# Hybrid attention in a decoder kernel: the output product of a batch's second half cut in two halves of 8 heads, in steps 3 and 4 of the next batch, in PSUM bank 7

## Chip, cores and metric

The kernel runs on one core of a Trainium2 chip. The metric is the device time of one execution in microseconds, lowest is best; several runs of each kernel are timed and their median is taken.

## What is computed

A two-layer decoder on x of shape (8, 256, 256). Six blocks, each on a layer-normed x and added back to it: a linear mixer, cross attention, a gated feed-forward, causal self attention, hybrid attention, and a mixture of experts. The change touches the fifth alone:

```python
# 16 query heads of 128, 4 key/value heads; T = 64 context tokens, L = 256 tokens
q = rope(rms_norm((x @ wq).reshape(B, L, 16, 128), q_norm_w))
k = rope(rms_norm((x @ wk).reshape(B, L, 4, 128), k_norm_w))
k_full = concat([rms_norm(ctx @ wk_ctx, k_norm_w), k]); v_full = concat([ctx @ wv_ctx, x @ wv])
scores = einsum("blhd,bmhd->bhlm", q, repeat(k_full, 4)) / sqrt(128) + mask
out = einsum("bhlm,bmhd->blhd", softmax(scores), repeat(v_full, 4)).reshape(B, L, 2048)
x = x + out @ wo          # the product this change moves: 2048 -> 256
```

## The kernel before

Each engine has a program of its own, written out by hand in order, and the engines meet at counting semaphores; nothing is scheduled by a tool. The phases run one after the other. The hybrid phase goes over the 8 batches in pairs (`over_pairs`: batch 0, then a loop of three rounds of two batches, then batch 7). In the functions `hybrid(b, par, nxt)`, one for each engine, a batch has 8 steps: step i = 4j + g treats token half j (128 rows) and key/value head g with its 4 query heads, numbered u = 8b + i over all batches. The batches are software-pipelined: in step i PE (TensorE) works at once on the raw queries of unit u+3, the transposed queries of u+2, the scores of u+1, the transposed probabilities of u-1 and the outputs of u-2, and in between on the keys and values of this batch and the next.

PE's order in a step (`hybrid` in the tensor block, L1861 on):

1. scores of u+1, tiles 0 and 1 (banks 3 and 4; wait on `e_mx`, DVE's maxima of the unit before, and on `e_qc`, ACT's copy of the turned queries);
2. a piece for the batch's keys or values in bank 2 (transposes of keys, `turn_keys`, in steps 5 and 6; a projection in step 3);
3. `raw_query(u+3)` in bank 1 (waits on `e_qa`, DVE's `rotate_query`, which reads that bank);
4. `outputs(u-2)` in bank 0;
5. a further piece in bank 2: in step 4 `hybrid_out(b-1, 1)`, in step 7 `hybrid_out(b, 0)`, the product with `wo` of the former batch's second half and of this batch's first half;
6. scores of u+1, tiles 2 and 3;
7. `turn_query(u+2)` in bank 2;
8. `turn_probs(u-1)` in banks 5, 6 and, from step 5 to step 0 of the next batch (units of j = 1), bank 7.

`hybrid_out` (L1800) is a chain of 16 products, one for each head, into `PS[:, 2, 0:D]`, and increments `e_y` at its end. As all the data is float32, each `product` (L1496, the helper through which nearly all matmuls go) is two MATMULs of the profile. DVE's `hybrid_finish` (L739) waits for `e_y`, adds the 128 x 256 sum to x (L742) and increments `s_x` for j = 1. Only then may bank 2 be written again: PE waits for `s_x` in step 4 before `turn_query`.

DVE's order in a step (`hybrid` in the vector block, L745 on): `turned_probs(u-2)` (L735 to L737), `masked_max(u+1)` of tiles 0 and 1 (L716), `finish_query(u+2)` (L698, L702), `normalise(u)` (L725, L728), the keys' pieces (`square_key` L600 in steps 2 to 4; `turn_key` L611 to L625, two of three in step 4 and one in step 5, for the next batch), in step 4 `hybrid_finish(b-1, 1)`, then `masked_max(u+1)` of tiles 2 and 3 (L716, L721), then `rotate_query(u+3)` (L686, L692). In batch 7 there is no next batch, so no keys' pieces. Batch 0 has no former batch, so no `hybrid_out(b-1, 1)`. After batch 7 the last `hybrid_out(7, 1)` stands alone. ACT copies the turned queries (L1364) and probabilities (L1380), takes the exponentials (L1373) and the squares (L1357), and copies the outputs into `eOT` (L1387). POOL computes the norms' scales.

Of the kernel before, what the change touches and what calls it, by code (L numbers as in the profile page):

```python
# [5 lines left out]
B, S, D = 8, 256, 256  # L6
P = 128
# [7 lines left out]
XH, XG, XD = 16, 4, 128  # L15
# [18 lines left out]
MIX, CROSS, FFN, SELF, HYBRID, MOE = range(6)  # L34


def decoder_kernel(nc, I, out, rows, results):
    F32, BF, U8, U32 = mybir.dt.float32, mybir.dt.bfloat16, mybir.dt.uint8, mybir.dt.uint32
    ALU, ACT, AX = mybir.AluOpType, mybir.ActivationFunctionType, mybir.AxisListType
    ds = bass.ds  # L40

    with ExitStack() as ctx:
# [3 lines left out]
        def sem(name):  # L46
            return ctx.enter_context(nc.semaphore(name))
# [43 lines left out]
        wo = sb("wo", [P, XH, D])  # L91
# [44 lines left out]
        PS = ctx.enter_context(nc.psum_tensor("PS", [P, 8, 512], F32))  # L136
# [16 lines left out]
        s_x = sem("s_x")  # L153
# [137 lines left out]
        eOT = cut(0, (XH, S), F32, early)  # L291
# [26 lines left out]
        f_slot = small[:, 264:280]; f_slotu = small[:, 280:296].bitcast(U32)  # L318
        f_tiles = small[0:NE, 296:297]; f_incl = small[0:NE, 297:298]
        f_ex = small[0:1, 304:304 + TILES]; f_exu = small[0:1, 368:368 + TILES].bitcast(U32)  # L320

        mark = {}

# [2 lines left out]
        def _(dve):  # L326
# [27 lines left out]
            def tokens(b, j):  # L354
                return X[:, ds(b, 1), j, :].rearrange("p a d -> p (a d)")
# [383 lines left out]
            def hybrid_finish(b, j):  # L739

                dve.wait_ge(e_y, J * b + j + 1)
                dve.tensor_tensor(tokens(b, j), tokens(b, j), PS[:, 2, 0:D], ALU.add)\  # L742
                    .then_inc(s_x if j else e_yf, 1)

            def hybrid(b, par, nxt):  # L745
# [139 lines left out]
            for b in range(B):  # L885
                for j in range(J):
                    i = J * b + j
# [606 lines left out]
        def _(pe):  # L1494
            def product(dst, lhs, rhs, first=True, last=True):
                return pe.matmul(dst, lhs, rhs, start=first, stop=last)  # L1496
# [31 lines left out]
            for c in range(C):  # L1528
                last = product(PS[:, 3 + c, 0:D], b_fold[:, c * P:(c + 1) * P], c_fold[:, :])
# [149 lines left out]
            def keys(b, par, k, at=2):  # L1679

                if k:
                    pe.wait_ge(s_xt, HYBRID * B + b + 1)
                else:
                    pe.wait_ge(e_ct, b + 1)
                for c in range(C):
                    if k:
                        last = product(PS[:, at, :], eXT[:, par, c, T + (k - 1) * P:T + k * P], wk[:, c, :],
                                       c == 0, c == C - 1)
                    else:
                        product(PS[T:P, at, :], eCT[:, c, :], wvc[:, c, :], c == 0, c == C - 1)  # L1690
                        last = product(PS[0:T, at, :], eCT[:, c, :], wkc[:, c, :], c == 0, c == C - 1)
                last.then_inc(e_k, 1)
# [102 lines left out]
            pe.wait_ge(d_yb, B - 1)  # L1795
            project_out(B - 1)

            def hybrid_out(b, j):

                pe.wait_ge(e_oc, 8 * b + XG * (j + 1))  # L1800
                for h in range(XH):
                    last = product(PS[:, 2, 0:D], eOT[:, h, j * P:(j + 1) * P], wo[:, h, :], h == 0, h == XH - 1)
                last.then_inc(e_y, 1)

            def values(b, par, k):

# [12 lines left out]
            def turn_query(v, i):  # L1819
                pe.wait_ge(e_qf, v + 1)  # L1820
                for h in range(GH):
                    last = pe.transpose(PS[:, 2, h * P:(h + 1) * P], eQA[:, i % 2, h * XD:(h + 1) * XD], ident[:, :])  # L1822
                last.then_inc(e_qt, 1)
# [37 lines left out]
            def hybrid(b, par, nxt):  # L1861
                former = type(b) is not int or b > 0
                more = nxt[0] == HYBRID
                for i in range(8):
                    u = 8 * b + i
                    further = [i + k < 8 or more for k in range(4)]
                    pars = [par if i + k < 8 else 1 - par for k in range(4)]
                    if further[1]:
                        scores(u + 1, (i + 1) % 8, pars[1], (0, 1))
                    if i < 7:  # L1870
                        pe.wait_ge(e_qc, u + 2)
                    if i == 0:
                        values(b, par, 0)
                    if i == 2:
                        xt_turn(*nxt, 2)
                    if i == 3 and more:
                        keys(nxt[1], 1 - par, 2)
                    if i == 5 and more:
                        turn_keys(nxt[1], 0)
                    if i == 6 and more:  # L1880
                        turn_keys(nxt[1], 2)
                    if further[3]:
                        raw_query(u + 3, (i + 3) % 8, pars[3])
                    if i == 2:
                        pe.wait_ge(s_twice, 48 * b + 48)
                    if i >= 2:
                        outputs(u - 2, i - 2, par)
                    elif former:
                        outputs(u - 2, i + 6, 1 - par)
                    if i == 0:  # L1890
                        pe.wait_ge(e_vr, 2 * b + 1)
                        values(b, par, 1)
                    if i == 1 and more:
                        keys(nxt[1], 1 - par, 0)
                    if i == 2 and more:
                        keys(nxt[1], 1 - par, 1)
                    if i == 4 and former:
                        hybrid_out(b - 1, 1)
                    if i == 5 and more:
                        pe.wait_ge(e_kc, 3 * b + 4)  # L1900
                        turn_keys(nxt[1], 1)
                    if i == 7:
                        hybrid_out(b, 0)
                    if further[1]:
                        scores(u + 1, (i + 1) % 8, pars[1], (2, 3))
                    if further[2]:
                        if i == 0:
                            pe.wait_ge(e_vr, 2 * b + 2)
                        if i == 1 and more:
                            pe.wait_ge(e_kr, 3 * b + 4)  # L1910
                        if i == 2 and more:
                            pe.wait_ge(e_kr, 3 * b + 5)
                        if i == 2 and not more:
                            pe.wait_ge(s_xt, MOE * B + 1)
                        if i == 3 and more:
                            pe.wait_ge(e_kr, 3 * b + 6)
                        if i == 4 and former:
                            pe.wait_ge(s_x, HYBRID * B + b)
                        if i == 5 and more:
                            pe.wait_ge(e_kc, 3 * b + 5)  # L1920
                        if i == 6 and more:
                            pe.wait_ge(e_kc, 3 * b + 6)
                        if i == 7:
                            pe.wait_ge(e_yf, b + 1)
                        turn_query(u + 2, (i + 2) % 8)
                    if i >= 1 or former:
                        turn_probs(u - 1, (i - 1) % 8)

# [138 lines left out]
```

## Time and profile before

| | us |
|---|---|
| Median of 3 runs | 1327.38 (1327.04 to 1330.12) |
| Profiled execution, its own time | 1331.08 |
| Its span, first to last instruction | 1329.3 |
| PE busy | 1080.0 (81%) |
| DVE busy | 884.6 (67%) |
| ACT busy | 625.3 (47%) |
| POOL busy | 318.7 (24%) |
| Mean granted PE clock | 0.914 of full |

The difference of 1.8 us between the profiled execution's own time and its span lies before the first and after the last instruction. The hybrid phase is the stretch from about 494 to 1149 us of the span. It is highly regular: from batch 1 to batch 6 each takes 81.4 or 81.5 us in the timeline, with a granted clock of 1.00 throughout, and batch 7 ends at 1149. The parts of the page that average over the whole span say little of it, so the views used below are those of a stretch: the busy time by stretch, the waits, and the timeline of each engine, in which the same step of two batches can be laid side by side.

### The profile page before, as it was taken

Reading aid. Unit: us, or ns where it says so; the run is one execution under the profiler, and the core shown is the slowest. Engines: PE = TensorE matmul, PEld = TensorE weight load, DVE = VectorE, ACT = ScalarE, POOL = GpSimd, SP = SyncE. Lnnn points to the kernel's source line nnn. Section 1 sums busy time; section 2 is a strip of 40 time slices with the busy share of each in tenths; the row PEclk is TensorE's granted clock in tenths of the full one; section 3 lists DMA queues with packets and bytes.
Section 4 is the critical chain, followed back from the end, with each engine's and each line's share of the span. In section 5 each row is a group of like instructions: output and inputs, shape, how many; then the busy total and the mean of one; then the engine's idle time right before and its main releaser. Section 6 shows DMA issues by size and latency. Waiting matters only on the chain.

```text
span 1329.3 us, 22376 instructions
## 1 busy us (share of the span) xinstructions
PE 1080.0 (81%) x6416; PEld 743.4 (56%) x6417; DVE 884.6 (67%) x2462; ACT 625.3 (47%) x1971; POOL 318.7 (24%) x467
## 2 busy tenths in 40 slices
PE   3677777788999958899999999999999999543790
PEld 2453444566666635566656666566665667332680
DVE  4576657588778756968778687886868776152352
ACT  1435676455555615555565455655546464031230
POOL 1113222113111322313132131321413210014334
PEclk9955899999999978899999999999999999855795
DMA  9400000112211000000000000000000000431455
GB/s 320 157 0 33 0 1 0 49 50 61 83 47 47 18 1 13 1 13 1 1 13 1 13 0 4 9 0 13 0 7 6 0 13 1 131 122 48 134 120 142
DMA packets 44549, 55.58 MB, mean 42 GB/s; under 512 B 4657, under 2 KB 35249, under 8 KB 44209
## 3 DMA queue, kind: packets, MB, share of 16 engines
q1 hardware_dynamic: 38576, 46.28, 11.4%
q10 hardware_dynamic: 4352, 4.20, 1.6%
q0 software_dynamic: 1536, 4.20, 1.0%
q8 instruction: 28, 0.46, 0.1%
q14 instruction: 57, 0.46, 0.1%
HBM read 34.73 MB, written 16.78 MB: 39 GB/s over the span
## 4 chain that ended last, share of the span: by engine, by line
PE 42%; DVE 7%; issue 4%; ACT 4%; DMA 2%; POOL 2%; ACTq 1%; SPq 0%; DVEq 0%; POOLq 0%
PE PS L1496 38%; PE PS L1822 2%; DMA rows_dram<-cosT 1%; ACT arena L1364 1%; PE PS L1845 1%; POOL rows_dram L1134 1%; ACT arena L1373 1%; DVE arena L692 1%; POOL arena L1149 1%; DVE early L869 1%; DVE arena L716 1%; DVE arena L728 1%; PE PS L1506 1%; SPq L958 0%; ACT arena L1480 0%
## 5 line engine op out<-in xcount | busy, mean ns | idle before, releaser
L1496 PE MATMUL PS<-EW,arena 128*64 (+5 forms) x1024 | 181.3, 319 | 25.0 <-DVE small L716 11.9
L1496 PEld LDWEIGHTS PS<-EW,arena 128*128 128x128 f32 (+1 forms) x1024 | 141.6, 163 | 63.0 <-issue 33.4
L1496 PE MATMUL PS<-early,arena 128*32 128x128 f32 (+6 forms) x864 | 107.9, 362 | 33.3 <-DVE early L579 23.7
L1496 PE MATMUL PS<-wq,EW 128*128 128x512 f32 x256 | 127.4, 621 | 7.7 <-DVE arena L692 7.1
L1098 POOL TENSOR_SCALAR small<-small 128x4 f32<-128x4 f32 x64 | 25.3, 396 | 424.2 <-ACT mask L1357 352.3
L716 DVE CUSTOM_DVE_ANT_0 arena<-PS,kmask 128x128 f32<-128x128 f32 (+3 forms) x256 | 93.8, 389 | 42.4 <-PE PS L1496 32.4
L1373 ACT ACTIVATE arena<-arena,small 128x128 f32<-128x128 f32 (+3 forms) x256 | 119.4, 471 | 0.3
L1496 PE MATMUL PS<-wo,early 128*128 128x256 f32 x512 | 113.2, 380 | 0.8 <-ACT early L1387 0.8
L1364 ACT ACTIVATE arena<-PS 128x512 f32<-128x512 f32 x64 | 38.2, 597 | 157.2 <-PE PS L1822 157.2
L1496 PEld LDWEIGHTS PS<-wo,early 128*128 128x128 f32 x512 | 97.4, 190 | 14.1 <-issue 1.2
L1000 POOL TENSOR_SCALAR ve<-mv 128x2 f32<-128x2 f32 x48 | 10.6, 221 | 369.3 <-DVE mv L351 369.2
L1496 PEld LDWEIGHTS PS<-early,arena 128*32 128x32 f32 (+3 forms) x864 | 51.0, 116 | 85.2 <-issue 46.1
L647 DVE TENSOR_REDUCE small<-PS 128x4 f32<-128x512 f32 x64 | 58.2, 951 | 42.0 <-PE PS L1496 42.0
L1357 ACT ACTIVATE mask<-PS 128x128 f32<-128x128 f32 x256 | 66.5, 273 | 40.0 <-PE PS L1496 39.6
L1496 PEld LDWEIGHTS PS<-wq,EW 128*128 128x128 f32 x256 | 45.8, 194 | 55.4 <-issue 41.2
L1100 POOL TENSOR_TENSOR small<-small,halves 128x4 f32<-128x4 f32 x64 | 72.8, 1138 | 5.3
L728 DVE TENSOR_SCALAR arena<-arena,small 128x128 f32<-128x128 f32 (+3 forms) x256 | 68.8, 333 | 2.3
L1496 PE MATMUL PS<-arena,EW 128*128 128x512 f32 (+1 forms) x160 | 63.2, 509 | 2.1 <-ACT arena L1380 2.1
L1338 ACT ACTIVATE arena<-PS,small 128x256 f32<-128x256 f32 x128 | 63.0, 492 | 0.0
L1506 PE MATMUL PS<-ident,XN 128*128 128x128 f32 x160 | 32.5, 339 | 37.2 <-DVE XN L365 37.2
L1299 ACT ACTIVATE early<-PS 128x384 f32<-128x384 f32 x64 | 28.5, 488 | 71.4 <-PE PS L1726 71.4
L742 DVE TENSOR_TENSOR X<-X,PS 128x256 f32 (+1 forms) x16 | 6.7, 421 | 81.1 <-PE PS L1496 81.1
(251 smaller groups left out, 2401.8 us busy)
## 6 DMA issues: line engine op xcount, KB each, us to landing
EW<-in_masksT_dram SPq DMA_DIRECT2D x32, 256.0 KB, 3.4
results_dram<-EW SPq DMA_DIRECT2D x32, 128.0 KB, 3.2
EW<-results_dram SPq DMA_DIRECT2D x4, 1024.0 KB, 9.5
rows_dram<-cosT SPq DMA_DIRECT2D x1, 4096.0 KB, 19.3
arena<-rows_dram SPq DMA_DIRECT2D x16, 256.0 KB, 3.1
results_dram<-early ACTq DMA_DIRECT2D x16, 256.0 KB, 3.2
X<-in_x_dram SPq DMA_DIRECT2D x1, 2048.0 KB, 8.9
wq<-in_wq_dram SPq DMA_DIRECT2D x1, 2048.0 KB, 10.9
```

What stands on the lines that cost most here:

```text
L647: last = dve.tensor_reduce(d_neg[:, i % 2, j, :], PS[:, 0:4, at:at + n], AX.X, ALU.max, negate=True)
L716: dve.tensor_tensor_reduce(probs(i, t), PS[:, 3 + t % 2, 0:n], kmask[:, at:at + n], 1.0, LOWEST, ALU.add, ALU.max, e_max[:, t:t + 1]).then ...
L728: last = dve.tensor_scalar(probs(i, t), probs(i, t), e_inv[:, t:t + 1], None, ALU.mult)
L1100: pool.tensor_tensor(e_rqs[:, i % 2, :], e_q3[:, i % 2, :], halves[:, 0:GH], ALU.pow).then_inc(e_rq, 1)
L1299: act.activation(dPT[:, i % 2, r, :], PS[:, 4 + r, 0:3 * P], ACT.Copy).then_inc(d_pt, 1)
L1338: act.activation(dP[:, i % 2, r, P:3 * P], PS[:, r, P:3 * P], ACT.Exp, bias=d_neg[:, i % 2, 1, r:r + 1]).then_inc(d_e, 1)
L1357: last = act.activation(eSQ[:, h * XD:(h + 1) * XD], PS[:, 1, h * XD:(h + 1) * XD], ACT.Square, accum_out=e_q2[:, i % 2, h:h + 1])
L1364: act.activation(eQT.rearrange("p (t h q) -> p h t q", t=4, h=GH), PS[:, 2, :].rearrange("p (h t q) -> p h t q", t=4, h=GH), ACT.Copy).the ...
L1373: last = act.activation(tile, tile, ACT.Exp, bias=e_neg[:, i % 2, t:t + 1], accum_out=e_sum[:, i % 2, t:t + 1])
L1496: return pe.matmul(dst, lhs, rhs, start=first, stop=last)
L1506: last = pe.transpose(PS[:, to, at:at + P], XN[:, j, c * P:(c + 1) * P], ident[:, :])
L1822: last = pe.transpose(PS[:, 2, h * P:(h + 1) * P], eQA[:, i % 2, h * XD:(h + 1) * XD], ident[:, :])
```

## The change

The product of a batch's second half, `hybrid_out(b-1, 1)`, no longer stands as one chain of 16 heads in step 4. Heads 0 to 7 are done in step 3 and heads 8 to 15 in step 4, at the same place in the step (after `outputs`, before the scores of tiles 2 and 3), and they accumulate in bank 7. DVE's `hybrid_finish` reads bank 7. PE's wait for `s_x` moves from step 4, before `turn_query`, to step 5, before `turn_probs`, the next to write bank 7. The first half's product (step 7) and the very last one (after batch 7) stay whole and in bank 2. DVE's, ACT's and POOL's orders are unchanged.

```diff
+        def out_bank(b, j):
+            return 7 if j and (type(b) is not int or b < B - 1) else 2
...
                 dve.wait_ge(e_y, J * b + j + 1)
-                dve.tensor_tensor(tokens(b, j), tokens(b, j), PS[:, 2, 0:D], ALU.add)\
+                dve.tensor_tensor(tokens(b, j), tokens(b, j), PS[:, out_bank(b, j), 0:D], ALU.add)\
...
-            def hybrid_out(b, j):
+            def hybrid_out(b, j, heads=range(XH)):
...
-                for h in range(XH):
-                    last = product(PS[:, 2, 0:D], eOT[:, h, j * P:(j + 1) * P], wo[:, h, :], h == 0, h == XH - 1)
-                last.then_inc(e_y, 1)
+                for h in heads:
+                    last = product(PS[:, out_bank(b, j), 0:D], eOT[:, h, j * P:(j + 1) * P], wo[:, h, :],
+                                   h == 0, h == XH - 1)
+                if heads[-1] == XH - 1:
+                    last.then_inc(e_y, 1)
...
+                    if i == 3 and former:
+                        hybrid_out(b - 1, 1, range(XH // 2))
                     if i == 4 and former:
-                        hybrid_out(b - 1, 1)
+                        hybrid_out(b - 1, 1, range(XH // 2, XH))
...
-                        if i == 4 and former:
-                            pe.wait_ge(s_x, HYBRID * B + b)
...
+                    if i == 5 and former:
+                        pe.wait_ge(s_x, HYBRID * B + b)
                     if i >= 1 or former:
                         turn_probs(u - 1, (i - 1) % 8)
```

The instructions on PE, first in step 3 of a loop batch, from `outputs` to the scores of tiles 2 and 3 (`wo` and `early` are the operands of the output product, `EW` and `arena` of the scores and outputs; L1499 of the changed kernel is L1496 of the one before). Before:

```order
L1496 MATMUL PS<-arena,EW 128x512 [waits e_oc,e_pta]
L1496 MATMUL PS<-arena,EW 128x256 [waits e_ptd]
L244 REGISTER_ALU [waits e_qc]
L1496 MATMUL PS<-EW,arena 128x320 [waits e_mx]
L244 REGISTER_ALU
L1496 MATMUL PS<-EW,arena 128x64 [waits e_mx]
L1496 MATMUL PS<-EW,arena 128x256
```

and now:

```order
L1499 MATMUL PS<-arena,EW 128x512 [waits e_oc,e_pta]
L1499 MATMUL PS<-arena,EW 128x256 [waits e_ptd]
L1803 ISA
L1499 MATMUL PS<-wo,early 128x256 [waits e_oc]
L1499 MATMUL PS<-wo,early 128x256 x7
L244 REGISTER_ALU [waits e_qc]
L1499 MATMUL PS<-EW,arena 128x320 [waits e_mx]
L244 REGISTER_ALU
L1499 MATMUL PS<-EW,arena 128x64 [waits e_mx]
L1499 MATMUL PS<-EW,arena 128x256
```

Eight products of `wo` (one with its wait, and 7) now stand between the outputs and the scores of tiles 2 and 3 of step 3. In step 4, from `outputs` to the first row of `turn_query` (L1822, now L1827), before:

```order
L1496 MATMUL PS<-arena,EW 128x512 [waits e_oc,e_pta]
L1496 MATMUL PS<-arena,EW 128x256 [waits e_ptd]
L1800 ISA
L1496 MATMUL PS<-wo,early 128x256 [waits e_oc]
L1496 MATMUL PS<-wo,early 128x256 x15
L244 REGISTER_ALU [waits e_qc]
L1496 MATMUL PS<-EW,arena 128x320 [waits e_mx]
L244 REGISTER_ALU
L1496 MATMUL PS<-EW,arena 128x64 [waits e_mx]
L1496 MATMUL PS<-EW,arena 128x256
L1918 REGISTER_ALU
L1822 MATMUL PS<-ident,arena 128x128 [waits e_qf,s_x]
```

and now:

```order
L1499 MATMUL PS<-arena,EW 128x512 [waits e_oc,e_pta]
L1499 MATMUL PS<-arena,EW 128x256 [waits e_ptd]
L1499 MATMUL PS<-wo,early 128x256 [waits e_oc]
L1499 MATMUL PS<-wo,early 128x256 x7
L244 REGISTER_ALU [waits e_qc]
L1499 MATMUL PS<-EW,arena 128x320 [waits e_mx]
L244 REGISTER_ALU
L1499 MATMUL PS<-EW,arena 128x64 [waits e_mx]
L1499 MATMUL PS<-EW,arena 128x256
L1827 MATMUL PS<-ident,arena 128x128 [waits e_qf]
```

Of the 16 products 8 are left, and `turn_query` no longer waits for `s_x`. In step 5, `turn_query` and `turn_probs` (L1845 and L1847, now L1850 and L1852), before:

```order
L1822 MATMUL PS<-ident,arena 128x128 [waits e_qf,e_kc]
L1822 MATMUL PS<-ident,arena 128x128 x3
L1845 MATMUL PS<-ident,arena 128x128 [waits e_p]
L1845 MATMUL PS<-ident,arena 128x128 x7
L1847 MATMUL PS<-ident,arena 128x128
```

and now:

```order
L1827 MATMUL PS<-ident,arena 128x128 [waits e_qf,e_kc]
L1827 MATMUL PS<-ident,arena 128x128 x3
L1932 REGISTER_ALU
L1850 MATMUL PS<-ident,arena 128x128 [waits e_p,s_x]
L1850 MATMUL PS<-ident,arena 128x128 x7
L1852 MATMUL PS<-ident,arena 128x128
```

The wait for `s_x` now stands at `turn_probs`.

## Rows read from the trace of the kernel before

**Rows 1.** Busy time by stretch: batch 4 of the hybrid phase, and batch 7.

```profile
core 0: us, PE busy (x) PEld busy (x) DVE busy (x) ACT busy (x) POOL busy (x), PEclk, DMA share, GB/s
...
822.90:904.40 81.50, 78.27 (x348) 52.53 (x347) 62.63 (x196) 43.60 (x165) 21.18 (x27) 1.00 0.02 5
...
1067.30:1149.00 81.70, 77.75 (x356) 55.43 (x353) 48.68 (x172) 39.11 (x136) 7.47 (x12) 1.00 0.02 6
```

**Rows 2.** Waits of PE in the hybrid phase: us in total, times, longest.

```profile
PE PS L1496 <- DVE small L716: 5.4, 7, 0.9
```

**Rows 3.** Timeline, PE, steps 3 to 6 of one steady batch.

```profile
start us, us, engine line op out<-in xcount [idle before <-releaser]
857.62 1.36 PE L1496 MATMUL PS<-EW,arena 128*128 128x320 f32 x6
...
864.40 7.07 PE L1496 MATMUL PS<-wo,early 128*128 128x256 f32 x32
871.30 1.36 PE L1496 MATMUL PS<-EW,arena 128*128 128x320 f32 x6
872.50 0.60 PE L1822 MATMUL PS<-ident,arena 128*128 128x128 f32 x4
...
873.94 1.12 PE L1496 MATMUL PS<-EW,arena 128*128 128x256 f32 x4 [0.30 <-ACT arena L1364]
...
875.38 1.98 PE L1496 MATMUL PS<-wq,EW 128*128 128x512 f32 x4
...
882.59 1.13 PE L1496 MATMUL PS<-EW,arena 128*128 128x256 f32 x4 [0.87 <-DVE small L716]
...
884.56 1.99 PE L1496 MATMUL PS<-wq,EW 128*128 128x512 f32 x4 [0.41 <-DVE arena L692]
```

**Rows 4.** Timeline, DVE, the same steps.

```profile
859.88 0.69 DVE L686 TENSOR_TENSOR arena<-PS,cosq 128x512 f32<-128x512 f32 x1
...
869.14 0.69 DVE L625 TENSOR_TENSOR early<-early,small 128x512 f32<-128x512 f32 x1
871.62 0.42 DVE L742 TENSOR_TENSOR X<-X,PS 128x256 f32 x1 [1.79 <-PE PS L1496]
...
874.83 0.27 DVE L736 COPY arena<-PS 64x128 f32<-64x128 f32 x1
...
876.86 0.69 DVE L702 TENSOR_TENSOR arena<-arena,small 128x512 f32<-128x512 f32 x1
877.97 0.18 DVE L725 RECIPROCAL small<-small 128x4 f32<-128x4 f32 x1 [0.43 <-ACT arena L1373]
...
882.04 0.48 DVE L716 CUSTOM_DVE_ANT_0 arena<-PS,kmask 128x320 f32<-128x320 f32 x1
...
884.42 0.68 DVE L735 COPY arena<-PS 128x512 f32<-128x512 f32 x1
```

**Rows 5.** Timeline, PE then DVE, step 6: DVE's paces behind PE.

```profile
888.53 1.36 PE L1496 MATMUL PS<-EW,arena 128*128 128x320 f32 x6
...
887.04 0.69 DVE L702 TENSOR_TENSOR arena<-arena,small 128x512 f32<-128x512 f32 x1
887.65 0.17 DVE L725 RECIPROCAL small<-small 128x4 f32<-128x4 f32 x1
...
890.79 0.69 DVE L686 TENSOR_TENSOR arena<-PS,cosq 128x512 f32<-128x512 f32 x1
```

**Rows 6.** Timeline, ACT, step 5: end of the exponentials.

```profile
877.75 0.19 ACT L1373 ACTIVATION_READ_ACCUMULATOR arena<-arena,small 128x1 f32 x1
```

**Rows 7.** Timeline, PE, batch 0, where no output product covers step 4.

```profile
546.99 2.02 PE L1496 MATMUL PS<-EW,arena 128*128 128x256 f32 x4 [3.59 <-DVE small L716]
```

**Rows 8.** Busy time by stretch, columns as in Rows 1, around that wait.

```profile
543.50:547.00 3.50, 0.01 (x1) 0.04 (x1) 3.43 (x9) 0.53 (x1) 2.93 (x3) 1.00 0.00 0
547.00:550.00 3.00, 3.00 (x9) 2.06 (x10) 2.92 (x13) 0.34 (x2) 0.00 (x0) 0.50 0.00 0
```

**Rows 9.** Timeline, DVE, step 4 of batch 7.

```profile
1109.18 0.42 DVE L742 TENSOR_TENSOR X<-X,PS 128x256 f32<-128x256 f32 x1 [6.37 <-PE PS L1496]
```

## Prediction

> **What bounds the kernel now.** I read the busy time by stretch first. In a steady batch of the hybrid phase PE is busy 78.27 us of 81.50 at a granted clock of 1.00, DVE 62.63 [rows 1]. PE sets the end, and only its 3.2 us of idle time a batch could be won; any new wait of PE is paid in full. Next the waits: PE waited 5.4 us in total, 7 times, for L716, DVE's masked maxima [rows 2]. Laid beside the timelines, that is 0.87 us once in each of six batches, at the start of step 6 [rows 3], and a smaller one in batch 7. Last the timelines of steps 3 to 6. In step 4 PE's output product runs from 864.40 to 871.30 [rows 3], 32 MATMULs in 6.90 us, so 0.216 us each. Beside it DVE works off its longest step: it ends with the keys' L625 at 869.14, and then idles 1.79 us for the end of the product, until L742 at 871.62 [rows 4]. So here PE covers DVE with 1.79 us to spare. From L742 on DVE is the late one: PE waits for it at 882.59 (0.87 us) and 884.56 (0.41 us) [rows 3].
>
> **PE's work.** The change removes no product and adds none: 16 MATMULs, 3.45 us, go from step 4 to step 3, and the product's end stays where it was, at 871.30, if PE meets no new wait. Splitting the chain costs no visible time: neighbouring groups start at the same pace within and across pieces [rows 3]. The changed kernel has six more rows on PE in all; at 0 us, since PE's registers and waits are worked off beside the matmuls, as in the unbroken run from 864.40 to 872.50 [rows 3].
>
> **The wait for `s_x`.** What the move could win is a wait of PE before `turn_query` in step 4. L742 ends at 871.62 + 0.42 = 872.04 [rows 4], while PE is at its scores until `turn_query` at 872.50, which shows no idle time before it [rows 3]. The wait was met 0.46 us early: the gain is 0. In its new place, before `turn_probs` of step 5, it stands behind the raw query, which comes 2.4 us or more after L742 by the times below. The Trainium skill (Perfetto Trace Analysis, Optimizing Tensor Performance, Matmuls) says that independent matmul groups should rotate through banks so that reading one out overlaps the next group. By that rule the move to bank 7 would help; the row shows no wait for it to remove, so the sum holds nothing for it.
>
> **DVE's start into step 4.** This is where the change costs. DVE's `masked_max` of tiles 2 and 3 in step 3 waits for PE's scores, and these now stand behind the first half: they start at 857.62 + 3.45 = 861.07 instead of 857.62 [rows 3]. Where DVE waited for these scores, its `rotate_query` (L686) began 890.79 - 888.53 = 2.26 us after they did [rows 5]. So it begins at 863.33, against 859.88 before [rows 4]: 3.45 us later, the full half. It idles that long in step 3, to no use. From there to L625 DVE ran without a wait before, and everything PE feeds it with in step 4 is 3.45 later too; so L625 starts at 872.59 instead of 869.14 [rows 4]. The next instruction can start 0.61 us after a 512-wide one (887.04 to 887.65 [rows 5]): L742 at 873.20, not 871.62. The product has been complete since 871.3. DVE is **1.58 us later** than before, since the half that left step 4 took its cover along and gave it to a step in which DVE had nothing to do.
>
> **From there to PE.** Before, L742 to L736 took 874.83 - 871.62 = 3.21 us with two short waits for the scores in it [rows 4]. Those waits vanish. L742 takes 0.34 us (0.42 less the 0.08 by which the next instruction overlaps its end, as with L702, 0.69 long and 0.61 to the next [rows 5]), and L716 to the end of `rotate_query` takes 884.42 - 882.04 = 2.38 us when nothing waits [rows 4]. L736 is at 873.20 + 2.72 = 875.92: 1.09 us late. Two things follow.
>
> PE in step 5. The scores of tile 0 need the maxima of tile 2. PE started 882.59 - 882.04 = 0.55 us after that L716 began [rows 3, 4]; now 873.54 + 0.55 = 874.09 against 873.94, 0.15 us late. The next `raw_query` needs `rotate_query`: in step 6 it came 884.56 - 884.42 = 0.14 us after DVE's next instruction [rows 3, 4]; now 876.06 against 875.38, 0.68 us late.
>
> DVE in step 5. L702 is at 876.86 + 1.09 = 877.95, and L725 could follow at 878.56. It began at 877.97 before, waiting for ACT's exponentials, which ended at 877.94 [rows 4, 6]. These are fed by PE and come at most 0.15 us later, so they no longer hold DVE: of the 1.09 us, **0.59** are left. Then DVE runs without a wait to L716 at 882.04 [rows 4], which is what PE waits for at 882.59. So PE starts step 6 **0.59 us later** than before, and as both are late by the same from there on, and no wait of PE in the rest of the batch is for something that was early, nothing wins it back.
>
> **How often, and the sum.** Batches 1 to 6 have both a former batch and the next batch's keys: 6 x 0.59 = 3.5 us. Batch 0 has no former batch and is untouched. In batch 7 DVE has no keys' work and idles 6.37 us before L742 [rows 9]; losing 3.45 us of it costs 0. The profiled execution's 1331.08 us (span 1329.3) would become 1334.6; it lies 3.7 us over the median, and the same 3.5 us on the median of 1327.38 give **1330.9 us**.
>
> **Check and bounds.** Batch 0 is the same step 4 without any cover: there PE waited 3.59 us for L716 at 546.99 [rows 7]. Half the cover, 3.45 us, brings that to 0.14, and the L742 that batch 0 lacks adds 0.34: a wait of 0.48 us at the start of step 5. My reckoning above has the 0.30 that is there now plus 0.15. The two agree to 0.03. The unknown is how much of the 1.09 is absorbed. Low end: 0.4 a batch, if PE's paces to DVE are 0.2 shorter than taken, 6 x 0.4 = 2.4. High end: 0.83, if the register work before L742, hidden in my sum, shows and ACT takes the 0.15 as well, 5.0. So 1329.8 to 1332.4 for this case. About 0.3%, 4.0 us, is what a measurement of this kernel can tell from no change, so the case lies on both sides of that line.
>
> **Rivals.**
> - *Nothing moves* (0 us, 1327.4). For: 1.79 us of idle time stood before L742, and some slack may exist which the profile doesn't show, or DVE may begin its step 4 earlier than in lockstep. Against: DVE's row of instructions is in order behind the scores of step 3.
> - *Faster.* If the shorter stretches let DVE finish the sum earlier relative to PE, the waits of 0.87 and 0.41 us in step 6 would go: 6 x 1.28 = 7.7 us, 1319.7. It would need the product to be complete before DVE is free, and DVE free before 871.62. The first comes true, the second can't, unless DVE's keys' work runs in the time won in step 3, and it stands behind the scores there.
> - *Nothing absorbed.* If ACT is later too (it copies the keys that PE turns in step 5), DVE's 1.09 or even 1.58 us come through: 6.5 to 9.5 us, 1333.9 to 1336.9. Against: ACT's input is only 0.15 us late.
> - *The clock falls.* After the wait of 3.59 us in batch 0, PE idle in 543.5 to 547, the granted clock was 0.50 (1.2 GHz) in 547 to 550 [rows 8]. If step 5's new waits did the same in each batch, with some 3 us at half speed, 1.5 us a batch would be added: 3.5 + 9 = 12.5, 1339.9. It decides from the point at which the waits of steps 5 and 6 pull the clock below 1.00. Against: the waits of 0.87 and 0.41 us, 2 us apart, left it at 1.00 [rows 1, 3], and the new ones, 0.45 and 0.53 us, are smaller. The Trainium skill (Perfetto Trace Analysis, Matmul Optimizations) says that the engine scales its power with utilization, so matmuls should run back to back in batches; it speaks against cutting one in two. The rows keep 2.4 GHz through gaps of that size, so I give it little.
>
> **How the numbers follow.** The forecast has 0.62, of which 0.25 lie over the 4.0 us line and 0.37 under it. Nothing moves 0.14, faster 0.09, nothing absorbed 0.09, the clock 0.06. So faster 0.09; same 0.37 + 0.14 = 0.51; slower 0.25 + 0.09 + 0.06 = 0.40. The range leaves out the faster case, the clock and the upper part of the unabsorbed one: 1327.0 to 1334.0, with the unchanged time just inside.
>
> **What would show it.** In a batch like the one above: DVE idle some 3 us before L716 in step 3; no idle time before L742 in step 4; PE idle about 0.45 us at the start of step 5 and about 0.5 us before the raw query after it, where there was none; no wait of DVE for the exponentials in step 5; a batch of 82.1 us instead of 81.5; a clock of 1.00. The reasoning is wrong if DVE still idles before L742, if the period of a batch doesn't grow, or if batch 7 changes by more than 0.3 us.

## The result, and the profile after

| | before | after |
|---|---|---|
| Median | 1328.81 us (13 runs) | 1332.76 us (13 runs) |
| Lowest and highest | 1326.73, 1332.12 | 1329.01, 1335.66 |
| Profiled execution's span | 1329.3 | 1328.6 |
| From the first to the last L742 (now L745) | 570.94 us | 574.36 us |

The ratio is 1.0027, with a 95% interval of 1.0015 to 1.0040: slower by 2.0 to 5.3 us. The spans of the two profiled executions say nothing of it: the one of the changed kernel reached the hybrid phase 3.9 us sooner (its first L745 is at 573.8, the first L742 at 577.65), and nothing that the change touches comes before that point. Within the hybrid phase the comparison is sharp, since the batches repeat to 0.1 us. Taken from one sum of a first half to the next (L742, L745), each of the six batches 1 to 6 took 81.42 us on average before and 81.99 now, 0.57 more, and batch 7 took 66.34 both times.

The busy time by stretch after, batch 4 and batch 7 (columns as in [rows 1]: PE, PEld, DVE, ACT and POOL busy, PEclk):

```profile
821.00:903.00 82.00, 78.26 (x347) 52.32 (x345) 62.41 (x195) 43.82 (x165) 19.50 (x27) 1.00 0.02 5
...
1066.90:1149.00 82.10, 78.09 (x356) 55.58 (x354) 49.08 (x173) 39.11 (x136) 7.48 (x12) 1.00 0.03 6
```

PE is as busy in batch 4 as in [rows 1], in a stretch of 82.00 us instead of 81.50, at a granted clock of 1.00. The timeline of PE after, the same batch as in [rows 3]; its step 3 begins at 849.81 where that of before begins at 851.93, so 2.12 us are to be added for a comparison:

```profile
855.49 3.62 PE L1499 MATMUL PS<-wo,early 128*128 128x256 f32 x16
858.95 1.36 PE L1499 MATMUL PS<-EW,arena 128*128 128x320 f32 x6
...
865.73 3.62 PE L1499 MATMUL PS<-wo,early 128*128 128x256 f32 x16
869.18 1.36 PE L1499 MATMUL PS<-EW,arena 128*128 128x320 f32 x6
870.37 0.60 PE L1827 MATMUL PS<-ident,arena 128*128 128x128 f32 x4
...
871.96 1.13 PE L1499 MATMUL PS<-EW,arena 128*128 128x256 f32 x4 [0.44 <-DVE small L719]
...
873.93 1.98 PE L1499 MATMUL PS<-wq,EW 128*128 128x512 f32 x4 [0.45 <-DVE arena L695]
...
881.03 1.13 PE L1499 MATMUL PS<-EW,arena 128*128 128x256 f32 x4 [0.78 <-DVE small L719]
...
883.01 1.98 PE L1499 MATMUL PS<-wq,EW 128*128 128x512 f32 x4 [0.41 <-DVE arena L695]
```

And DVE's, as in [rows 4]:

```profile
859.85 0.49 DVE L719 CUSTOM_DVE_ANT_0 arena<-PS,kmask 128x320 f32<-128x320 f32 x1 [3.14 <-PE PS L1499]
...
861.21 0.69 DVE L689 TENSOR_TENSOR arena<-PS,cosq 128x512 f32<-128x512 f32 x1
...
870.47 0.69 DVE L628 TENSOR_TENSOR early<-early,small 128x512 f32<-128x512 f32 x1
871.08 0.41 DVE L745 TENSOR_TENSOR X<-X,PS 128x256 f32 x1
...
873.79 0.27 DVE L739 COPY arena<-PS 64x128 f32<-64x128 f32 x1
...
876.43 0.17 DVE L728 RECIPROCAL small<-small 128x4 f32<-128x4 f32 x1
...
880.49 0.48 DVE L719 CUSTOM_DVE_ANT_0 arena<-PS,kmask 128x320 f32<-128x320 f32 x1
```

The product now stands in two chains of 16 MATMULs, at 855.49 and 865.73. DVE waits 3.14 us for the scores of step 3 (L719 at 859.85), and up to the sum no more: `hybrid_finish` (L745) at 871.08 follows L628 with no idle time, where L742 waited 1.79 us in [rows 4]. PE waits 0.44 us for DVE at the start of step 5 (871.96) and 0.45 us before the raw query (873.93), where it had 0.30 and nothing; step 6 begins at 881.03, at 883.15 on the clock of before, 0.56 us late.

### The profile page after: what moved, and what is told of

Its sections match the earlier page's. It is cut to its first block, busy times and chain, and to the rows that moved or that the text cites. A ratio compares the mean times of both kernels' runs of the same rounds, so it can differ in the third digit from the quotient of the medians.

```text
span 1328.6 us, 22367 instructions
## 1 busy us (share of the span) xinstructions
PE 1075.8 (81%) x6407; PEld 741.0 (56%) x6417; DVE 883.4 (66%) x2462; ACT 626.7 (47%) x1971; POOL 308.9 (23%) x467
## 3 DMA queue, kind: packets, MB, share of 16 engines
q1 hardware_dynamic: 38576, 46.28, 11.4%
## 4 chain that ended last, share of the span: by engine, by line
PE 36%; DVE 10%; issue 10%; ACT 3%; POOL 1%; SPq 1%; DMA 1%; ACTq 0%; DVEq 0%; POOLq 0%
PE PS L1499 33%; DVE arena L719 1%; PE PS L1827 1%; DVE arena L695 1%; DVE arena L731 1%; PE PS L1850 1%; POOL arena L1152 1%; ACT arena L1367 1%; DVE early L872 1%; DVE arena L705 1%; DVE early L625 1%; DVE early L620 1%; DVE arena L701 1%; DVE early L616 1%; SPq L961 0%
## 5 line engine op out<-in xcount | busy, mean ns | idle before, releaser
L1499 PE MATMUL PS<-EW,arena 128*64 (+5 forms) x1024 | 181.1, 319 | 25.6 <-DVE small L719 14.0
L1499 PEld LDWEIGHTS PS<-EW,arena 128*128 128x128 f32 (+1 forms) x1024 | 141.0, 163 | 64.0 <-issue 33.6
L719 DVE CUSTOM_DVE_ANT_0 arena<-PS,kmask 128x128 f32<-128x128 f32 (+3 forms) x256 | 93.6, 389 | 63.6 <-PE PS L1499 54.6
L1499 PE MATMUL PS<-wq,EW 128*128 128x512 f32 x256 | 127.3, 620 | 10.4 <-DVE arena L695 9.8
L1499 PE MATMUL PS<-early,arena 128*32 128x256 f32 (+6 forms) x856 | 104.1, 358 | 34.1 <-DVE early L582 23.7
L1101 POOL TENSOR_SCALAR small<-small 128x4 f32<-128x4 f32 x64 | 18.0, 281 | 420.3 <-ACT mask L1360 345.0
L1499 PE MATMUL PS<-wo,early 128*128 128x256 f32 x512 | 114.3, 379 | 0.8 <-ACT early L1390 0.8
L1499 PEld LDWEIGHTS PS<-wo,early 128*128 128x128 f32 x512 | 97.2, 190 | 14.3 <-issue 1.2
L1499 PEld LDWEIGHTS PS<-early,arena 128*32 128x32 f32 (+3 forms) x864 | 50.4, 115 | 83.5 <-issue 44.0
L1499 PEld LDWEIGHTS PS<-wq,EW 128*128 128x128 f32 x256 | 45.7, 193 | 58.6 <-issue 41.3
L1499 PE MATMUL PS<-arena,EW 128*128 128x512 f32 (+1 forms) x160 | 63.2, 509 | 2.1 <-ACT arena L1383 2.1
L1340 ACT ACTIVATE arena<-PS,small 128x128 f32<-128x128 f32 x128 | 48.8, 381 | 25.1 <-DVE small L650 24.4
```

Of the source, the lines that this page charges most:

```text
L719: dve.tensor_tensor_reduce(probs(i, t), PS[:, 3 + t % 2, 0:n], kmask[:, at:at + n], 1.0, LOWEST, ALU.add, ALU.max, e_max[:, t:t + 1]).then ...
L1340: act.activation(dP[:, i % 2, r, 0:P], PS[:, r, 0:P], ACT.Exp, bias=d_neg[:, i % 2, 0, r:r + 1])
```

## Experiments

The theory is that of the prediction, called the cover theory in what follows. Its rivals: bank 7 or the new place of the wait costs the 0.6 us; cutting the chain does, wherever it is cut. A third reading, that each head moved costs something, comes up on the way. Each expectation is quoted as it was written before the run. Lines of the experiments' kernels are those of the changed kernel unless said otherwise. "A batch" is the time from one sum of a first half to the next, in the run's profile, over batches 1 to 6.

| run | batch, us | median (before beside it) | ratio to before, 95% interval |
|---|---|---|---|
| before | 81.42 | | |
| the change, 8 and 8 | 81.99 | 1332.76 (1328.81) | 1.0027 (1.0015 to 1.0040) |
| whole in step 4, bank 7 | 81.40 | 1330.00 (1329.47) | 1.0007 (0.9996 to 1.0018) |
| 4 and 12 | 81.77 | 1330.01 (1329.47) | 1.0014 (1.0001 to 1.0027) |
| 6 and 10 | 81.41 | 1328.87 (1329.14) | 1.0000 (0.9989 to 1.0011) |
| 12 and 4 | 84.10 | 1344.78 (1329.47) | 1.0112 (1.0086 to 1.0138) |
| 16 in step 3 | 85.95 | 1356.87 (1329.47) | 1.0203 (1.0180 to 1.0226) |
| 8 and 8, a key piece in step 3 | 81.40 | 1329.31 (1329.14) | 1.0002 (0.9991 to 1.0012) |
| 4 and 12, POOL's order changed | 81.41 | 1329.77 (1329.35) | 1.0004 (0.9994 to 1.0014) |
| steps 4 and 5, 8 and 8 | 80.06 | 1319.85 (1329.14) | 0.9933 (0.9916 to 0.9950) |
| steps 4 and 5, 10 and 6 | 79.73 | 1316.75 (1329.14) | 0.9912 (0.9894 to 0.9929) |
| steps 4 and 5, 12 and 4 | 80.01 | 1318.34 (1329.35) | 0.9919 (0.9906 to 0.9932) |

### Bank 7 and the wait alone

```diff
-                    if i == 3 and former:
-                        hybrid_out(b - 1, 1, range(XH // 2))
                     if i == 4 and former:
-                        hybrid_out(b - 1, 1, range(XH // 2, XH))
+                        hybrid_out(b - 1, 1)
```

> All 16 heads in step 4 as before, but in bank 7, DVE reading bank 7 and PE's wait for s_x before turn_probs of step 5. Cover theory (the moved heads take PE's cover away from DVE's longest step): nothing of DVE's order in time changes, so the same time as before within 1 us, a batch of 81.4 to 81.5 us, DVE idle 1.79 us before the sum. Bank theory (writing and reading bank 7, or the wait's new place, costs the 0.58 us a batch): 82.0 us a batch, +3.5 us.

A batch takes 81.40 us. DVE idles 1.78 us before the sum, as it did before. PE's waits in this run, counted from 570 us on, behind batch 0's step 4 (us in total, times, longest):

```profile
PE PS L1499 <- DVE small L719: 5.4, 7, 0.9
PE PS L1499 <- DVE arena L695: 4.5, 13, 0.4
```

The first is [rows 2] to the tenth, which leave out batch 0 too (its wait of 3.59 us is [rows 7]); the second was the same 4.5, 13 and 0.4 in the kernel before. So neither bank 7 nor the wait's place costs anything that shows, and neither wins anything: the wait in step 4 had hidden nothing, as [rows 3] had shown at 872.50.

### Four heads, and a surprise

```diff
-                        hybrid_out(b - 1, 1, range(XH // 2))
+                        hybrid_out(b - 1, 1, range(4))
...
-                        hybrid_out(b - 1, 1, range(XH // 2, XH))
+                        hybrid_out(b - 1, 1, range(4, XH))
```

> As the change, but 4 heads in step 3 and 12 in step 4. Cover theory: DVE is 4 x 0.431 = 1.73 us later in step 4 and had 1.79 us to spare, so DVE's sum comes when it came before and the time is that of before within 1 us (81.5 us a batch, DVE idle under 0.2 us before the sum). Theory that the cut itself costs (a second chain, its own waits and registers): the same 0.58 us a batch as the change, +3.5 us.

A miss for both: 81.77 us, 0.35 over before, where the cover theory said 0 and the cut 0.58. The timeline of DVE in this run shows where it comes from:

```profile
858.27 0.63 DVE L724 TENSOR_SCALAR small<-small 128x4 f32<-128x4 f32 x1
...
868.82 0.42 DVE L745 TENSOR_TENSOR X<-X,PS 128x256 f32 x1
```

L724, the negation of 4 numbers for each row, takes 0.63 us; the median of the 48 in batches 1 to 6 of the changed kernel is 0.17. POOL's timeline beside it, in the same run:

```profile
856.83 1.04 POOL L1096 TENSOR_TENSOR small<-small,halves 128x4 f32<-128x4 f32 x1
857.84 1.04 POOL L1089 TENSOR_TENSOR early<-early 128x512 f32<-128x512 f32 x1
```

L724 began at 858.27 and ended at 858.90, and POOL's L1089, the squares of the third key piece, ran to 858.88. The negation didn't end before POOL was through. In all six batches the negation of step 3 takes 0.63 or 0.64 us. PE then waited for `rotate_query` before its raw query of step 4, which it had not done before:

```profile
858.82 1.13 PE L1499 MATMUL PS<-EW,arena 128*128 128x256 f32 x4 [0.30 <-ACT arena L1367]
...
860.21 1.98 PE L1499 MATMUL PS<-wq,EW 128*128 128x512 f32 x4 [0.26 <-DVE arena L695]
```

The raw query follows the scores of step 4 by 1.39 us, where the changed kernel (862.61 - 861.59) and the one before have 1.02: the 0.37 us are the batch's 0.35. The scores of step 3 are what starts DVE there, and moving them by 1.73 us put the negation beside an instruction of POOL that used to come after it. Two runs test this reading. The first moves two more heads, the second moves the same four and changes only POOL's order:

```diff
-                        hybrid_out(b - 1, 1, range(4))
+                        hybrid_out(b - 1, 1, range(6))
...
-                        hybrid_out(b - 1, 1, range(4, XH))
+                        hybrid_out(b - 1, 1, range(6, XH))
```

> As the change, but 6 heads in step 3 and 10 in step 4. The run with 4 and 12 had a batch of 81.8 us instead of 81.4, and in it the small negation after the maxima of step 3 took 0.63 us instead of 0.17, ending with POOL's squares of a key. Theory of a collision with POOL (one of the two engines waits while the other's instruction runs): with 6 heads the negation comes 0.9 us later and POOL is through, so there is no collision; DVE is 2.59 us later in step 4, 0.72 us at the sum, 0.23 us after the rotated query, which the 0.43 us wait for ACT takes up: 81.4 to 81.5 us a batch, less than with 4 heads moved although more was moved. Theory that each head moved costs, or the cut does: a period between those of 4 and 8 heads, 81.8 to 82.0 us.

81.41 us, so moving 6 heads costs nothing where moving 4 cost 0.35. DVE's timeline in this run bears the expectation out:

```profile
862.77 0.17 DVE L724 TENSOR_SCALAR small<-small 128x4 f32<-128x4 f32 x1
...
872.82 0.41 DVE L745 TENSOR_TENSOR X<-X,PS 128x256 f32 x1
...
878.46 0.18 DVE L728 RECIPROCAL small<-small 128x4 f32<-128x4 f32 x1 [0.21 <-ACT arena L1376]
```

The negation takes 0.17 us. The sum of the first half was at 822.38 here and at 821.90 before, so 872.82 stands against 872.10: the sum is 0.72 us late. The two short waits for scores behind the sum, worth 3.21 - 2.72 = 0.49 us in the prediction's own reckoning, are gone and take that much of it. And at 878.46 DVE waits 0.21 us for ACT instead of 0.43: the 0.23 us that are left go into a wait that was there anyway.

```diff
                     if i == 3 and more:
-                        key_scales(nxt[1], 1)
                         key_squares(nxt[1], 2)
+                        key_scales(nxt[1], 1)
```

> 4 heads in step 3 and 12 in step 4 as in the run that had a batch of 81.8 us, and on POOL the squares of the third key piece (1.04 us) ahead of the scales of the second one (0.23 and 1.04 us) instead of behind them, both in step 3. The squares now run some 1.3 us earlier, before DVE's small negation. Collision theory, squares alone: the negation takes 0.17 us and a batch 81.4 us. Collision theory, any of POOL's instructions: the power of the scales now runs where the squares ran, the negation still takes about 0.7 us and a batch 81.8 us or a little more. Theory that each head moved or the cut costs: 81.8 us, with a negation of 0.17 us.

The kernel is the 4 and 12 of the miss, with this one swap in POOL's order. A batch takes 81.41 us. The timeline of DVE in this run:

```profile
858.92 0.17 DVE L724 TENSOR_SCALAR small<-small 128x4 f32<-128x4 f32 x1
```

That of POOL, in the same run:

```profile
857.05 1.04 POOL L1089 TENSOR_TENSOR early<-early 128x512 f32<-128x512 f32 x1
...
858.49 1.04 POOL L1096 TENSOR_TENSOR small<-small,halves 128x4 f32<-128x4 f32 x1
```

The negation of 858.92 lies inside POOL's L1096 (858.49 to 859.53), the power of the key scales, and takes its 0.17 us, as it does in all six batches. So it isn't any instruction of POOL that stops it, but the squares. Why these and not the power isn't settled: the one reads and writes 512 elements in each row, the other 4. Nor does the reading fit without a remainder: a negation in step 2 of the changed kernel begins at 848.91 and takes 1.28 us, to 850.19; POOL's squares there run from 849.12 to 850.15 by the trace, so it was held 0.21 us before they are shown to begin, with a power (848.11 to 849.14) still under way. Three of the six batches show this; in the other three the negation begins at the power's end and takes 1.03 to 1.05 us, to the end of the squares. The bounds of POOL's instructions may be off by that much, or a power may hold DVE in its last part; no run here decides it. The Trainium skill (SBUF — State Buffer, SBUF: two separate sides) says that the port pair shared by VectorE and GpSimd is an exclusive lock: of a GpSimd instruction and a VectorE instruction in a 2-port mode, or one with two SBUF inputs against a GpSimd instruction that reads SBUF, whichever starts first holds it for the whole instruction. The negation has one input, in SBUF, and no run here shows its mode. The squares agree with the lock, the negation's end being that of L1089 to 0.02 us; the power, beside which it isn't held up, does not.

### More heads

```diff
-                        hybrid_out(b - 1, 1, range(XH // 2))
+                        hybrid_out(b - 1, 1, range(12))
...
-                        hybrid_out(b - 1, 1, range(XH // 2, XH))
+                        hybrid_out(b - 1, 1, range(12, XH))
```

> As the change, but 12 heads in step 3 and 4 in step 4. Cover theory: DVE is 1.73 us later than in the change, all of it past the point where its slack is used up: PE waits some 2.2 us at the start of step 5, a batch takes 82.0 + 1.7 = 83.8 us, so 6 x 2.3 = +13.9 us over before, at a clock of 1.00. Theory that the cut itself costs: +3.5 us as in the change. If a wait of some 2 us pulls the clock below 1.00, more than +13.9.

The ratio of 1.0112 is 14.9 us. The timeline of PE in this run, step 5:

```profile
880.97 1.13 PE L1499 MATMUL PS<-EW,arena 128*128 128x256 f32 x4 [2.17 <-DVE small L719]
...
882.94 3.59 PE L1499 MATMUL PS<-wq,EW 128*128 128x512 f32 x4 [0.45 <-DVE arena L695]
```

The wait is 2.17 us, as worked out. What is new is the raw query behind it: 3.59 us, where [rows 3] has 1.98 for the same four MATMULs. The busy time by stretch of the same run shows why:

```profile
core 0: us, PE busy (x) PEld busy (x) DVE busy (x) ACT busy (x) POOL busy (x), PEclk, DMA share, GB/s
878.70:881.00 2.30, 0.13 (x2) 0.03 (x1) 2.23 (x7) 0.76 (x2) 1.56 (x2) 1.00 0.00 0
...
883.00:886.00 3.00, 3.00 (x4) 1.45 (x5) 2.89 (x11) 1.98 (x8) 0.00 (x0) 0.50 0.00 0
886.00:889.00 3.00, 3.00 (x14) 1.90 (x13) 2.93 (x8) 2.23 (x10) 1.01 (x2) 0.96 0.00 0
```

After the wait PE's granted clock was 0.50, its level of 1.2 GHz, in the stretch of the raw query, and back near 1.00 in the next. The clock fell after this wait in each of the six batches, which took 83.7 to 84.9 us. The third sentence of the expectation came true by the trace, where six batches took 6 x 2.68 = 16.1 us more than before instead of 13.9; the medians alone, at 11.4 to 18.3, can't tell. The fall adds little, because a slow PE gives DVE time to catch up: PE's wait of 0.78 us for DVE at the start of step 6 is gone (the scores at 890.74 follow at once).

```diff
-                        hybrid_out(b - 1, 1, range(XH // 2))
+                        hybrid_out(b - 1, 1)
...
-                    if i == 4 and former:
-                        hybrid_out(b - 1, 1, range(XH // 2, XH))
```

> All 16 heads in step 3, none in step 4. Cover theory: PE waits about 3.59 + 0.34 = 3.9 us for DVE at the start of step 5 of each batch, as in batch 0, and 6 x 4.04 = +24 us in all at a clock of 1.00. In batch 0 a wait of 3.59 us was followed by a granted clock of 0.50: if that happens in each batch, PE's next steps run at half speed and each batch loses 1.5 to 3.5 us more, +33 to +45 us. Theory that the cut itself costs: there is no cut, so the time of before.

The timeline of PE in this run:

```profile
890.87 1.50 PE L1499 MATMUL PS<-EW,arena 128*128 128x256 f32 x4 [3.89 <-DVE small L719]
```

The busy time by stretch, columns as above:

```profile
891.00:893.00 2.00, 2.00 (x9) 1.12 (x9) 1.95 (x8) 0.00 (x0) 0.00 (x0) 0.62 0.00 0
893.00:896.00 3.00, 3.00 (x5) 1.39 (x6) 2.82 (x10) 2.54 (x10) 0.00 (x0) 0.68 0.00 0
```

The scores behind the wait take 1.50 us instead of 1.13, the mark of the lower clock. PE waits 3.89 us at the start of step 5; batch 0's 3.59 [rows 7] with the sum's 0.34 added are 3.93. The ratio of 1.0203 is 27.0 us (23.9 to 30.0), and six batches in the trace took 27.2 more than before: the 24 of the lateness, and 3 for the clock where 9 to 21 had been expected. So the clock fell as expected and cost less, as the half speed again takes the place of a later wait. And there is no cut in this kernel, so a cut isn't needed for the loss; that a cut by itself costs nothing is what 6 and 10 showed, and the next run.

### Work for DVE in the time it was given

```diff
+                    if i == 3 and nxt[0] == HYBRID:
+                        turn_key(nxt[1], 0)
                     if i == 4:
                         if nxt[0] == HYBRID:
-                            turn_key(nxt[1], 0)
                             turn_key(nxt[1], 1)
```

> The change, and on DVE the keys' first piece, turn_key(0) (two instructions, 1.32 us from start to start), moved from step 4 to step 3, ahead of the maxima of tiles 2 and 3, where DVE idles 3.14 us in the change. Cover theory: DVE reaches the sum 1.32 us earlier in step 4, so the 0.58 us a batch go and the period is 81.4 to 81.5 us, the time of before; PE's new waits at the start of step 5 and before its raw query vanish. Theory that the cut itself costs: still 82.0 us a batch.

81.40 us and a ratio of 1.0002: the same two halves of 8 heads, and nothing lost. The timeline of DVE in this run:

```profile
854.24 0.67 DVE L614 TENSOR_TENSOR early<-early,kw 64x512 f32<-64x512 f32 x1
854.94 0.68 DVE L628 TENSOR_TENSOR early<-early,small 64x512 f32<-64x512 f32 x1
857.47 0.49 DVE L719 CUSTOM_DVE_ANT_0 arena<-PS,kmask 128x320 f32<-128x320 f32 x1 [1.84 <-PE PS L1500]
...
867.38 0.41 DVE L745 TENSOR_TENSOR X<-X,PS 128x256 f32 x1
```

L614 and L628, the first key piece, are done at 854.24 to 855.6, in step 3, and DVE still waits 1.84 us for the scores behind them. PE, in the same run, has the 0.30 us for ACT at the start of step 5 as before and no wait before the raw query:

```profile
869.43 1.13 PE L1500 MATMUL PS<-EW,arena 128*128 128x256 f32 x4 [0.30 <-ACT arena L1368]
...
870.88 1.98 PE L1500 MATMUL PS<-wq,EW 128*128 128x512 f32 x4
```

This is the plainest proof of the cover theory, since PE's program is that of the change to the last instruction. (There is one line more in this kernel, but the lines of DVE up to here are the same.)

### The cut in the other direction

If step 4 has too much cover and step 5 too little, heads should go from step 4 to step 5. DVE's sum goes with them.

```diff
-                    if i == 3 and former:
-                        hybrid_out(b - 1, 1, range(XH // 2))
                     if i == 4 and former:
-                        hybrid_out(b - 1, 1, range(XH // 2, XH))
+                        hybrid_out(b - 1, 1, range(10))
...
                         turn_keys(nxt[1], 1)
+                    if i == 5 and former:
+                        hybrid_out(b - 1, 1, range(10, XH))
...
-                        if former:
-                            hybrid_finish(b - 1, 1)
                     if i == 5 and nxt[0] == HYBRID:
                         turn_key(nxt[1], 2)
+                    if i == 5 and former:
+                        hybrid_finish(b - 1, 1)
```

> The cut in the other direction: 10 heads in step 4 and 6 in step 5, after the keys' second piece, DVE's sum in step 5, after its key piece. Cover theory: step 4 has 1.79 us too much cover and step 5 too little, since DVE's last key piece makes PE wait 0.87 and 0.41 us at step 6. DVE then starts on the maxima of step 4 at once, PE's waits of 0.87 us for the maxima and 0.41 us for the query in step 6 go (0.30 us for ACT stays in place of the first): 1.4 us less a batch, a period of 80.0 us, 6 x 1.4 = -8.6 us. Theory that cutting costs: slower than before.

79.73 us a batch, 1.69 less than before, and a ratio of 0.9912 (0.9894 to 0.9929), so 11.7 us less. The timeline of PE in this run, steps 4 to 6:

```profile
858.52 4.48 PE L1499 MATMUL PS<-wo,early 128*128 128x256 f32 x20
...
865.48 1.13 PE L1499 MATMUL PS<-EW,arena 128*128 128x256 f32 x4 [0.30 <-ACT arena L1367]
...
866.92 1.98 PE L1499 MATMUL PS<-wq,EW 128*128 128x512 f32 x4
...
870.47 2.75 PE L1499 MATMUL PS<-wo,early 128*128 128x256 f32 x12
...
875.57 0.27 PE L1852 MATMUL PS<-ident,arena 128*128 128x128 f32 x1
875.70 1.12 PE L1499 MATMUL PS<-EW,arena 128*128 128x256 f32 x4
...
877.10 1.88 PE L1499 MATMUL PS<-wq,EW 128*128 128x512 f32 x4
```

The waits of 0.87 and 0.41 us in step 6 [rows 3] are gone: step 6 begins at 875.70, before the last transpose of step 5 has ended. The expectation of 1.4 us was larger than its own terms, 0.87 and 0.41 less the 0.30 that were to stay for ACT, and these 0.30 don't show either. By starts, up to the last transpose of step 5 the batch is as before; the scores of step 6 follow it by 0.13 us instead of 1.15, the raw query follows them by 1.40 instead of 1.97, and the piece behind that by 1.72 instead of 1.82. That makes 1.69. Batch 7, which the expectation didn't name, is 0.66 us shorter too, 65.68 against 66.34: PE's 0.19 us wait for DVE at the start of its step 6 is gone, and it comes sooner to the transposes of step 5 (1.20 us after the scores instead of 1.47). The same with 8 and 8:

```diff
-                        hybrid_out(b - 1, 1, range(10))
+                        hybrid_out(b - 1, 1, range(8))
...
-                        hybrid_out(b - 1, 1, range(10, XH))
+                        hybrid_out(b - 1, 1, range(8, XH))
```

> As the last, with 8 heads in step 4 and 8 in step 5. Cover theory: step 4 is now 0.34 us short of cover at the raw query of step 5 and the rest is as with 10 and 6: 1.07 us less a batch than before, a period of 80.4 us, -6.4 us. Theory that cutting costs: slower than before.

80.06 us, 1.36 less than before, where 1.07 had been expected; like 10 and 6 it came out 0.3 us better. It is 0.33 more than with 10 and 6, and this difference was expected at 0.34. It stands where the expectation had it: PE waits 0.26 us for DVE before the raw query of step 5 (866.89), which comes 1.78 us after the step's scores instead of 1.44. And with 12 and 4:

```diff
-                        hybrid_out(b - 1, 1, range(10))
+                        hybrid_out(b - 1, 1, range(12))
...
-                        hybrid_out(b - 1, 1, range(10, XH))
+                        hybrid_out(b - 1, 1, range(12, XH))
```

> 12 heads in step 4 and 4 in step 5, DVE's sum in step 5. With 10 and 6 a batch took 79.7 us, with 8 and 8 80.0 us. Cover theory: with 12 in step 4 DVE waits for PE in step 4 again, but only 0.7 us, and in step 5 its last key piece ends about 1 us after the product, at the edge of making PE wait in step 6: 79.7 us a batch as with 10 and 6, at most 0.3 us more. Theory that more work moved from step 4 to step 5 is better throughout: worse than 10 and 6, 80.0 us or more.

80.01 us, where the two readings of the expectation meet; that 8 and 8, with more moved to step 5, was worse than 10 and 6 speaks against more being better throughout. DVE comes to the sum without waiting for the rest of the product; its timeline in this run shows no idle time before L745:

```profile
871.73 0.41 DVE L745 TENSOR_TENSOR X<-X,PS 128x256 f32 x1
```

The sum ends at 872.14, and PE's `turn_probs` of step 5, which has the wait for `s_x`, begins at 872.20:

```profile
872.20 1.09 PE L1850 MATMUL PS<-ident,arena 128*128 128x128 f32 x8
```

In this run, and in none of the others with a product in step 5, PE waits there for the sum (L745), 1.7 us in six times; it begins 0.65 us after `turn_query` instead of 0.44 with 10 and 6, which is 0.21 of the 0.28 us between the two batches. So 10 and 6 lies at the bottom: 8 and 8 leaves too little cover in step 4, and with 12 and 4 the sum comes too late for PE in step 5. By the trace it is the fastest of all the kernels run; the medians of 10 and 6 and 12 and 4 don't tell the two apart. It beats both the kernel before and the change.

## Why the prediction was right

**The wait for `s_x` and bank 7, 0 us.** Right, and shown alone by the first experiment. The rule on rotating banks that the prediction takes from the Trainium skill (Perfetto Trace Analysis, Optimizing Tensor Performance, Matmuls) had nothing to work on here, since nobody waited for bank 2.

**DVE's start into step 4, 1.58 us late.** Right to the hundredth: L745 at 871.08 is 873.20 on the clock of before, as worked out. The step on which all hung, that DVE is in order behind the scores of step 3, showed as the 3.14 us wait at 859.85.

**From there to PE.** Worked out were 0.45 us of idle time at the start of step 5, 0.15 of it new, and the raw query at 876.06; measured 0.44, and 873.93 + 2.12 = 876.05. The exponentials no longer held DVE (L728 at 876.43 with no idle time). PE's step 6 was to be 0.59 us late and was 0.56; a batch grew by 0.57 us.

**The sum.** 6 x 0.59 = 3.5 us; six batches gave 3.4 us in the trace, the runs 2.0 to 5.3. Batch 7 didn't change, as said. The medians differ by 3.95 us; the median of before itself moved from 1327.38 (3 runs) to 1328.81 (13 runs), which is 1.4 of the 1.9 us by which the forecast of 1330.9 lies under the 1332.76 measured. That shift also puts the measured median 0.4 us above the 1329.8 to 1332.4 that the prediction gave for its own case; as a difference, 3.95 lies within its 2.4 to 5.0. The half microsecond between the 3.4 us of the trace and the 3.95 of the medians is less than the interval can resolve.

**What the prediction didn't see.** It named no collision between DVE and POOL, and with 8 heads there was none. With 4 there was, and it made the same reasoning wrong by 0.35 us a batch, so it was luck that the forecast for 8 heads met none. That 1.79 us of slack was room for 4 heads was true of DVE and PE alone. Beyond it, DVE's wait of 0.43 us for ACT made room for 6.

**The rivals.** Nothing absorbed is out: DVE's 1.09 us shrank to 0.57 as the 0.43 us wait for ACT went. Faster is out for this change, but what it named, the waits of 0.87 and 0.41 us in step 6, is what the cut in the other direction won. The clock rival is real and needed more: gaps of 0.44, 0.45 and 0.78 us left it at 1.00, waits of 2.17 and 3.89 us did not.

## What to carry to other kernels

A long piece of PE's work that waits for nobody is cover for the engine beside it; before one is moved, look at what that engine does in the same step, and whether it has anything to do in the step to which the piece goes. Here 1.79 us of idle time before the sum and 1.28 us of PE's waits in step 6 said in the same rows that the cover belonged later, not earlier. How much later is bounded by who reads the result: with 12 heads in step 4 and 4 in step 5, PE came to wait for the sum. And after a shift of a microsecond look at small instructions for a sudden long one: a third engine may stand in the way.

## What was unexpected of the hardware

A DVE instruction on 4 elements a row, 0.17 us otherwise, took 0.63 us beside POOL's product of 512 elements a row, and ended with it. It wasn't new: in the kernel before and in the change the one of step 1 takes 0.90 us (840.35 after) and the one of step 2 1.03 to 1.28 us (848.91 after). There PE's next pieces wait for ACT or for nothing, so no cost of it shows. POOL's power on 4 elements a row, 1.04 us long itself, didn't do that to a negation in its middle. In the kernel before, POOL's powers themselves take 1.44 or 1.45 us instead of 1.04 where DVE's pieces of the keys run beside them (at 866.55 and 868.55, for instance); no run tests why.

The fall of the clock cost little: 3 us in all over six batches with 16 heads in step 3. In the batch shown there, scores and raw query of step 5 take 4.84 us (890.87 to 895.71) instead of 3.27 (873.94 to 877.21 before), 1.57 more; but the scores of step 6 then follow the last transpose by 0.17 us instead of 1.15. PE at half speed does its waiting while it works.
